# A gated cross-attention block: in the slot stage, maxima and sums over all slots are taken on VectorE, and the stage opens in another order

## The reference

```python
x = _layernorm(_layernorm(x)) * norm_g + norm_b           # 64 x 64 tokens
se = _layernorm(slot_embeds) * scale                      # 16 experts x 64 slots
logits = einsum('bnd,esd->bnes', x, se)
dispatch = softmax(logits, axis=1)                        # over the 64 tokens of a batch
combine = softmax(logits.reshape(B, N, -1), axis=-1)      # over all 1024 slots
slots = einsum('bnd,bnes->besd', x, dispatch)
gate = gelu(einsum('besd,edf->besf', slots, Wg) + bg)
up = einsum('besd,edf->besf', slots, Wu) + bu
eout = einsum('besf,efo->beso', gate * up, Wd) + bd
out = einsum('bns,bso->bno', combine, eout.reshape(B, E*S, -1))
x = x + tanh(g_ffn[0]) * out
```

## Time and profile before

| what | us |
|---|---|
| median of 3 runs (1504.78 to 1507.92) | 1505.92 |
| the profiled execution | 1507.57 |
| its span on the core | 1505.9 |
| PE busy | 1382.3 (92%) |
| DVE busy | 953.9 (63%) |
| ACT busy | 1013.6 (67%) |
| POOL busy | 524.3 (35%) |

### The profile page before, as it was taken

How to read it: one execution, slowest core, us unless ns; L and a number is a source line. 1 busy time by engine, 2 the same in 40 slices (tenths; PEclk the granted TensorE clock), 3 DMA queues, 4 the chain that set the end, 5 groups by cost and what they waited for, 6 DMA issues and landing times. The chain is left out here.

```text
span 1505.9 us, 33716 instructions
## 1 busy us (share of the span) xinstructions
PE 1382.3 (92%) x12029; PEld 1174.7 (78%) x12029; DVE 953.9 (63%) x2374; ACT 1013.6 (67%) x2019; POOL 524.3 (35%) x510
## 2 busy tenths in 40 slices
PE   5898699899999999999999999988999999877895
PEld 4887588788888888888888888876788888655673
DVE  6998766766766767677667666543455555644455
ACT  5887587577676776776776767647788888534442
POOL 3112355322322323223223223212235555545553
PEclk9999899999999999999999999999999999979998
DMA  8300100499930000000000000040000000122236
GB/s 222 85 1 1 58 2 1 87 183 84 114 17 2 2 1 2 2 2 1 2 2 1 2 2 2 1 114 15 1 31 15 16 16 19 31 63 69 70 92 175
DMA packets 124980, 60.46 MB, mean 40 GB/s; under 512 B 41945, under 2 KB 120241, under 8 KB 124690
## 3 DMA queue, kind: packets, MB, share of 16 engines
q1 hardware_dynamic: 120274, 48.92, 18.4%
q0 software_dynamic: 4544, 9.38, 1.9%
HBM read 28.84 MB, written 29.44 MB: 39 GB/s over the span
## 5 line engine op out<-in xcount | busy, mean ns | idle before, releaser
L1349 DVE SCALAR_TENSOR_TENSOR hidden<-psU,b_cols,gelu 128x512 f32<-128x512 f32 x256 | 191.6, 750 | 170.5 <-ACT gelu L1474 95.6
L1474 ACT ACTIVATE gelu<-psG,b_cols 128x512 f32<-128x512 f32 x256 | 176.5, 689 | 110.1 <-PE psG L142 97.2
L1296 POOL TENSOR_TENSOR combine_sum<-combine_sum,combineT 128x512 f32<-128x512 f32 x48 | 63.4, 1322 | 294.7 <-ACT combineT L1488 294.7
L1325 POOL TENSOR_TENSOR dispatchT<-dispatchT,dispatch_inv 128x512 f32<-128x512 f32 x64 | 67.8, 1060 | 232.5 <-DVE dispatch_inv L1453 232.5
L1608 PE MATMUL psU<-w_down,hidden 128*64 128x128 f32 x2048 | 123.4, 273 | 0.0
L1608 PE MATMUL psDown<-w_down,hidden 128*64 128x128 f32 x2048 | 122.7, 273 | 0.0
L1861 POOL TENSOR_TENSOR probs<-probs,row_sum 128x512 f32<-128x512 f32 x64 | 66.4, 1037 | 143.5 <-DVE row_sum L1974 142.6
L1608 PEld LDWEIGHTS psU<-w_down,hidden 128*64 128x64 f32 x2048 | 113.2, 137 | 1.3 <-issue 1.2
L1608 PEld LDWEIGHTS psDown<-w_down,hidden 128*64 128x64 f32 x2048 | 113.9, 137 | 0.1
L140 PE MATMUL psG<-slots_hi,w_gate_hi 128*128 128x512 f32 x256 | 106.4, 416 | 0.5 <-DVE slots_lo L1435 0.5
L2038 ACT ACTIVATE probs<-psS,neg_max 128x128 f32<-128x128 f32 x256 | 91.4, 385 | 22.8 <-DVE neg_max L1971 16.8
(11 more groups left out here) (406 smaller groups left out, 3624.8 us busy)
## 6 DMA issues: line engine op xcount, KB each, us to landing
sorted_x<-empty_rows SPq DMA_DIRECT2D x1, 12736.0 KB, 76.5
tile_rows<-sorted_x SPq DMA_DIRECT2D x78, 65.0 KB
sorted_x<-empty_rows SPq DMA_DIRECT2D x1, 4544.0 KB, 30.3
expert_ys<-expert_y SPq DMA_DIRECT2D x16, 256.0 KB, 3.7
x<-in_x SPq DMA_DIRECT2D x8, 256.0 KB, 5.9
ctx<-in_ctx SPq DMA_DIRECT2D x8, 256.0 KB, 5.9
w_gate_raw<-in_L_ffn_Wg SPq DMA_DIRECT2D x1, 2048.0 KB, 10.6
w_up_raw<-in_L_ffn_Wu SPq DMA_DIRECT2D x1, 2048.0 KB, 15.8
```

Source lines behind the costliest of these rows:

```text
L1325: pool.tensor_tensor(e[:], e[:], over(rb[:], SEQ, 2), ALU.mult).then_inc(s["eb_normed"], 1)
L1349: dve.scalar_tensor_tensor(hid[e][:, half, :], U[half][:], bcol[:, 1, 4 * ch + 2 * e + half:][:, 0:1], gel[half][:], ALU.add, ALU.mult).th ...
L1474: act.activation(gel[half][:], G[half][:], ACT.Gelu, bias=bcol[:, 0, 4 * ch + 2 * e + half:][:, 0:1]).then_inc(s["gelu"], 1)
```

## The change

- The maxima over slots: the four transposes, the four spreading matmuls and ScalarE's copy go. VectorE turns `top` in blocks of 32x32 and reduces each (`max_quadrants`, at the end of chunk 6), then brings the four quadrants of the partitions together, spreads the result over the quadrants and turns it back (`max_rows`, at the start of chunk 7).
- The sums over slots: the matmuls against ones go. VectorE turns and reduces `combine_sum` the same way (`sum_quadrants` before expert_out of chunk 7, `sum_inverse` near the end of that chunk).
- The waits of the next octet's first products for these results go.
- Scores 6 and 7 are both made in chunk 6, none in chunk 7.
- The next octet's tokens are turned at the start of chunk 1 (in octet 0: chunk 2), into psM.
- The opening: scores need no slots first; VectorE does the dispatch work before the running maxima, which come last, all seven (`first_top`), and `max_rows` for octet 0 stands in its chunk 0, behind the first two hidden. x_hat for octet 1 comes late in chunk 0 of octet 0.
- 24 of the statistics of 32 tiles go to the end of the first attention (four were there already), four stay in the stage.

```diff
+                    dve.wait_ge(s["bn"], OP * (OCTETS - 1))
+                    for t in range(OP, PAIRS - OP):
+                        dve.bn_aggr(c.stats[:, t, :], c.bn[:, t, :]).then_inc(s["late_aggr"], 1)
...
-    AHEAD = ((), (), (0,), (1, 2), (3,), (4, 5), (6,), (7,))
+    AHEAD = ((), (), (0,), (1, 2), (3,), (4, 5), (6, 7), ())
...
-            x_stats(c, dve, s["aggr"])
+            for t in range(PAIRS - OP, PAIRS):
+                dve.bn_aggr(c.stats[:, t, :], c.bn[:, t, :]).then_inc(s["aggr"], 1)
...
+            def by_quadrant(source, turned, n, op, count):
+                dve.transpose(turned[:], source).then_inc(s[n + "_turned"], 1)
+                need(dve, s[n + "_turned"], count)
+                dve.tensor_reduce(quad[n][:, 0, :], turned[:].rearrange("p (b i) -> p b i", i=32), AX.X, op
+                                  ).then_inc(s[n + "_quad"], 1)
+            def together(n, out, done, op, count):
+                need(dve, s[n + "_quad"], count)
+                for q in range(1, Q):
+                    last = dve.tensor_copy(quad[n][0:32, q, :], quad[n][32 * q:32 * (q + 1), 0, :])
+                last.then_inc(s[n + "_together"], 1)
+                need(dve, s[n + "_together"], count)
+                dve.tensor_reduce(out, quad[n][0:32].rearrange("p q b -> p b q"), AX.X, op).then_inc(s[done], 1)
+                need(dve, s[done], count)
+            def first_top():
+                for n in range(1, CH):
+                    need(dve, s["first_top"], n - 1)
+                    dve.tensor_tensor(top[:], raw[:, 0, :] if n == 1 else top[:], raw[:, n, :], ALU.max
+                                      ).then_inc(s["first_top"], 1)
+                dve.wait_ge(s["first_top"], CH - 1)
+            def max_quadrants(o):
+                need(dve, s["lb_max"], 8 * (o + 2))
+                need(dve, s["ct_sub"], 8 * (o + 1))
+                need(dve, s["mtok"], o + 1)
+                by_quadrant(top[:], mb, "max", ALU.max, o + 2)
+            def max_rows(o):
+                need(dve, s["mb_ready"], o + 1)
+                together("max", mtok[0:32, :], "mtok", ALU.max, o + 2)
+                for q in range(1, Q):
+                    last = dve.tensor_copy(mtok[32 * q:32 * (q + 1), :], mtok[0:32, :])
+                last.then_inc(s["max_spread"], 1)
+                need(dve, s["max_spread"], o + 2)
+                dve.transpose(mb[:].rearrange("p (b i) -> p b i", i=32), over(mtok[:], 32, 2)).then_inc(s["mb_ready"], 1)
+            def sum_quadrants(o):
+                need(dve, s["ct_summed"], 7 * (o + 1))
+                need(dve, s["max_turned"], min(o + 2, OCTETS))
+                need(dve, s["dtok"], o)
+                by_quadrant(total[:].rearrange("p t n -> p (t n)"), top, "sum", ALU.add, o + 1)
+            def sum_inverse(o):
+                need(dve, s["den"], o)
+                together("sum", dtok[0:32, :], "dtok", ALU.add, o + 1)
+                need(dve, s["x_new"], o)
+                for q in range(Q):
+                    last = dve.tensor_copy(ra[32 * q:32 * (q + 1), :],
+                                           dtok[0:32, :].rearrange("p (t q) -> p t q", q=Q)[:, :, q])
+                last.then_inc(s["den"], 1)
+                need(dve, s["den"], o + 1)
+                dve.reciprocal(ra[:], ra[:]).then_inc(s["den_inv"], 1)
+                need(dve, s["den_inv"], o + 1)
+                dve.tensor_scalar(ra[:], ra[:], c.gates[:, 1:2], None, ALU.mult).then_inc(s["den_gated"], 1)
...
+                    if ch == CH - 1 and has_head(o) and has_core(o):
+                        max_rows(o)
+                    if ch == turned_at(o) and has_head(o) and has_core(o):
+                        need(dve, s["lnT_hi"], o + 1)
+                        need(dve, s["lb"], 8 * (o + 1))
+                        dve.tensor_tensor(lnT[1][:], M[:, 1, :], lnT[0][:].bitcast(F32), ALU.subtract
+                                          ).then_inc(s["lnT_lo"], 1)
                     if not has_core(o):
+                        if exists(o, ch, 3):
+                            shift_dispatch(o, ch)
                         for n in ahead(o, ch):
                             column_max(o, n)
+                            if n == 5:
+                                slots_low(o, ch)
+                        if exists(o, ch, 3):
+                            sum_dispatch(o, ch)
+                        if ch == CH - 1:
+                            first_top()
+                            max_quadrants(o)
+                        continue
+                    if ch == 0 and has_head(o) and o > 0:
+                        x_hats(o)
+                    hidden(k, 0, ch, 0)
+                    hidden(k, 0, ch, 1)
+                    if ch == 0 and o == 0:
+                        max_rows(-1)
...
+                        if ch == CH - 1:
+                            sum_quadrants(o)
                         expert_out(k, 0, ch)
+                    if ch == 0 and o == 0:
+                        x_hats(o)
                     if exists(o, ch, 1):
+                        slots_low(o, ch)
+                    if has_core(o) and has_head(o) and ch == CH - 2:
+                        max_quadrants(o)
                     if has_core(o) and ch == CH - 1:
+                        sum_inverse(o)
                     if exists(o, ch, 3):
+                        sum_dispatch(o, ch)
...
+                    if ch == turned_at(o) and has_head(o) and has_core(o):
+                        need(pe, s["x_normed"], o + 1)
+                        need(pe, s["sl_lo"], 2 * (k + 1))
+                        for t in range(OP):
+                            last = pe.transpose(M1[:, t, :], xn[1 - par][:, t, :], c.ident[:])
+                        last.then_inc(s["tx"], 1)
...
-                first = isinstance(k, int) and ch == 0 and e == 0
-                if first:
-                    need(pe, s["mtok"] if half == 0 else s["mb_ready"], k // CH + 1)
+                if isinstance(k, int) and k == 0 and e == 0:
+                    pe.wait_ge(s["raw"], CH)
...
-                        for t in range(OP):
-                            last = pe.transpose(G0[:, t, :], top[:, t * P:(t + 1) * P], c.ident[:])
-                        last.then_inc(s["top_t"], 1)
...
-                        for t in range(OP):
-                            last = pe.matmul(U[0][:, t:t + 1], total[:, t, :], ones[:], start=True, stop=True)
-                        last.then_inc(s["den"], 1)
...
-                        for t in range(OP):
-                            last = pe.matmul(G[1][:, t * P:(t + 1) * P], mtok[:, t:t + 1].to_broadcast([P, P]), ident_r[:],
-                                             start=True, stop=True)
-                        last.then_inc(s["mb"], 1)
```

More of the change, by code:

```diff
@@ L1208, in stage_experts0 @@
         top = sb("top_over_chunks", [P, OT])
-        mtok, mb = sb("max_c", [P, OP], F32R), sb("max_c_row", [P, OT])
-        ident_r = sb("ident_rounded", [P, P], F32R)
+        quad = {n: sb(f"{n}_by_quadrant", [P, Q, OT // 32]) for n in ("max", "sum")}
+        mtok, mb = sb("max_c", [P, OT // 32]), sb("max_c_row", [P, OT])
+        dtok = sb("sum_c", [P, OT // 32])
         eb = [sb(f"dispatchT{i}", [P, OB, SEQ]) for i in range(2)]
@@ L1254, in second, with turned_at @@
             return any(n in group[1:] for group in AHEAD)
+        def turned_at(o):
+            return 2 if isinstance(o, int) and o == 0 else 1
         def score_bank(o, n):
@@ L1362, in column_max @@
                 if n == 1:
-                    need(dve, s["top_t"], o + 1)
-                if n > 0:
+                    need(dve, s["sum_quad"], o)
+                if n > 0 and has_core(o):
                     need(dve, s["lb_max"], j)
@@ new lines, in x_hats, with shift_dispatch @@
+            def x_hats(o):
+                need(dve, s["x_normed"], o)
+                for p in range(OP):
+                    t = 4 * (o + 1) + p
+                    last = dve.tensor_scalar(xh[:, p, :], c.x[:, t, :], c.stats[:, t, 0:1],
+                                             c.inv[:, bass.ds(t, 1)], ALU.subtract, ALU.mult)
+                last.then_inc(s["x_hat"], 1)
+            def shift_dispatch(o, ch):
+                k = o * CH + ch
+                n = (ch + 3) % CH
+                need(dve, s["raw"], k + 4)
+                need(dve, s["lb_max"], k + 4)
+                need(dve, s["td"], k + 2)
+                dve.tensor_tensor(eb[(ch + 1) % 2][:], raw[:, n, :].rearrange("p (b n) -> p b n", b=OB),
+                                  over(nm[:, n, :], SEQ, 2), ALU.add).then_inc(s["shifted"], 1)
@@ new lines, in sum_dispatch, with slots_low @@
+            def sum_dispatch(o, ch):
+                k = o * CH + ch
+                need(dve, s["eb_exp"], k + 4)
+                need(dve, s["eb_normed"], k + 3)
+                dve.tensor_reduce(rb[:], eb[(ch + 1) % 2][:], AX.X, ALU.add).then_inc(s["eb_sum"], 1)
```

(22 more changed lines are left out.)

130 lines of the change are left out of this document (41 added, 89 removed).

## The result

The changed kernel takes 1533.02 us (median of 4 runs, 1532.36 to 1533.81) against 1506.26 of the kernel before beside it: ratio 1.0176, interval 1.0163 to 1.0189, slower. 1515.4 was predicted, 1500 to 1530 given as the range. The profiled execution has a span of 1531.3 us against 1505.9: 25.4 us more, where I had 9.5.

What follows compares the result with a forecast made beforehand. VectorE's chain was taken to be as long as TensorE's work at the ends of octets 1 to 5. Ends 3.0, chunk 7 10.2, octet 6 -2.27, last sums -0.9, transposes -1.0, opening 0.5: +9.5, 1515.4 us, range 1500 to 1530.

Steps and rivals of the forecast that it cites:

- the stall of chunk 7: Chunk 7, seven times: TensorE waits for hidden behind VectorE's maxima work and copies held beside GpSimd, 1.45 us each, 10.2 together.
- the longer chain at an octet's end: From expert_out of chunk 7 to chunk 0's first hidden, VectorE's chain grows by 0.50 us, six ends, 3.0 together.
- the falls of the clock: Rival, 12%: after the new 2.7 us pauses TensorE's clock falls in each of five octets, 8.5 us, giving 1524.
- tokens' transposes: Turning the next octet's tokens at a chunk's start saves perhaps 0.15 us, seven times, 1.0 together.
- opening: Start of the slot block: b_cols comes at about the same time, +0.5 us, bounds -2 and +2.
- last sums: Eighth octet, without successor: only the sums' matmuls leave TensorE, 0.9 us saved.
- the end of octet 6: No x_hat follows since octet 7 prepares nothing, so the 2.27 us removed from TensorE is kept as gain.
- Removed from TensorE, 2.27 an end: Between chunk 7 and the next chunk 0, three removed groups cost TensorE 2.27 us in each of seven octets.
- The rival that no stall arises: Rival, 15%: VectorE's transposes and copies fit in chunk 7, only chunk 0 loses: -0.7 us, 1505.
- the one that TensorE stays the bound: Rival, 13%: TensorE's removed work is time saved, 17.3 us less, 1488.6.
- the one that x_hat gets free of GpSimd: Rival, 8%: x_hat no longer runs beside GpSimd, 3.47 becomes 1.11 us, five ends gain 2.3 each: 1504.
- The end of octet 0: The routing constants' chain starts from VectorE's row sums too, so this end also costs +0.50 us.

Runs made afterwards that it cites:

- e8: Changed kernel with its two new small buffers last and 480 unused bytes, so slots and hidden stand where the kernel before has them: 1530.18 us, ratio 1.0155.
- e9: e8, e2 and e3 together, x_hat behind the first expert_out of chunk 0, tokens turned at chunk 2 in every octet: 1501.91 us, ratio 0.9971.
- e3: Changed kernel with max_rows behind the first two hidden of chunk 7 instead of ahead of them: 1523.79 us, ratio 1.0097.
- e5: Changed kernel with the edits of e2, e3 and e4 together: 1514.6 us, ratio 1.004.
- e2: Changed kernel with sum_inverse moved from the end of chunk 7 into the next octet's chunk 0, just ahead of its use: 1517.18 us, ratio 1.0055.
- e1: Changed kernel with 32 unused bytes ahead of the slots, bringing slots and hidden to multiples of 64 bytes: 1535.74 us, ratio 1.0183.
- e4: Changed kernel with x_hat behind the first two hidden of chunk 0 instead of ahead of them: 1519.26 us, ratio 1.0067.
- e7: Kernel before with 96 unused bytes ahead of dispatchT, so operands stand at the changed kernel's addresses: 1515.04 us, ratio 1.0051.
- e10: Kernel before with 512 unused bytes ahead of dispatchT: ratio 1.0007.
- e11: Kernel before with 64 unused bytes ahead of dispatchT: ratio 1.0016.
- e12: Kernel before with 96 unused bytes between the slots and gelu, so only gelu, hidden and expert_out move: ratio 0.9998.
- e6: Kernel before, unedited, profiled a second time: 1506.39 us, ratio 0.9994.

## Why the prediction was wrong

The sign, the places and the two chains were right. What failed were two terms of the sum and one that was put at nothing: the stall of chunk 7 was 1.98 and not 1.45 us, the longer chain at an octet's end cost 1.03 and not 0.50 and also reached a wait that I had not listed, and the pitch of the products, which the sum did not have, cost 5.8. With the ends at their measured size alone the sum would have given about 1523; the pitch and the falls of the clock, which I had only as a rival, took it past 1530. The account of the profiled executions, by chunk lengths:

| part | predicted | measured |
|---|---|---|
| ends of octets, tokens' transposes included, at equal pitch | +9.9 | +17.5 |
| pitch of the products | none | +5.8 |
| clock after the pauses | 12% rival | +3.0 |
| opening, from the first score to the first chunk 1 | +0.5 | -0.1 |
| last sums | -0.9 | -0.2 |
| stages ahead and behind | none | -0.5 |
| sum | +9.5 | +25.5 |

Worked out, with e8 for the changed kernel at equal pitch: its chunks 6, 7 and 0 (13.11 + 13.66 + 15.19) less those of before (12.39 + 14.66 + 11.88) are 3.03 at an end where the clock holds; chunk 1 gives 0.31 back (12.11 against 12.42). That is 13.6 for five such ends; 1.0 for the end of octet 6, 2.7 for that of octet 0 and 0.2 for the transposes in octet 0's chunk 2 make 17.5 (for octet 0 with octet 1's chunk 0 as long as in the changed kernel, since e8's is 0.5 longer). Pitch: 0.7 in each of seven octets and 0.9 in the last. Stages: the first score comes 0.7 later (156.47 against 155.81), and from the first router transpose to the end it is 505.94 against 507.06. The spans to one digit give 25.4.

- **Removed from TensorE, 2.27 an end: right.** Before, chunk 7 takes 14.66 and a chunk with one score and no reduction 12.39: 2.27. In e9 chunks 7 and 0 take 23.65; before 26.54, of which 0.71 was the score: 2.18 less, with 0.2 to 0.3 of waiting left on either side.
- **VectorE's transposes and reductions, 0.71 and 0.60: right** (0.74 from 593.48 to 594.22, 0.60 to the row behind at 594.82). The copies beside GpSimd's normalization were held, as predicted from x_hat: 0.90 for three, 0.52 in e3 without it. The rule cited from the Trainium skill ("SBUF — State Buffer", section "SBUF: two separate sides") is borne out for small copies by e5, where a copy of 0.16 us lasted 1.17 and ended with GpSimd's instruction.
- **The stall of chunk 7, 1.45: too small by 0.5.** At equal pitch chunk 7 takes 13.66 (e8) where a chunk without score or wait takes 11.68: 1.98. The wait of 1.50 costs 1.78 of it, and the late expert_out, of which I had listed no consumer in this chunk, 0.15. `max_rows` alone is 1.71 (e3). The rival that no stall arises is out, as are the one that TensorE stays the bound and the one that x_hat gets free of GpSimd: it took 3.44 (610.58).
- **The chain of the sums, +0.50: the other term that was mis-sized.** From expert_out to the end of the first hidden I had 8.26 + 0.50; it is 605.36 to 614.65 = 9.29, so +1.03. I took 0.1 for a small instruction that waits for nobody; they start 0.17 apart (four in 0.68 and three in 0.52), and the chained ones 0.21 to 0.28. That is 1.9 from 607.27 to 609.18 where I had 1.44. The upper bound that I wrote beside it (1.1) was nearly the true value. The two terms close the account of an end: 1.98 + 1.03 = 3.01, where the chunks give 3.03 and I had 1.45 + 0.50.
- **A wait not listed.** My chain led to hidden alone. It passes expert_out, and TensorE's second group of psU products, which needs it, comes some 2.2 us after a chunk's first product, before the one that needs hidden. Hence 0.53 at 610.72, and 0.88 at the end of octet 6. There I had written that 2.27 is kept, since no x_hat follows. Chunk 0 took 12.94; 11.79 with the sums out of the way (e2). With the stall of chunk 7 I had -0.8 for this end; it cost 1.0.
- **The end of octet 0: too small in the same way.** Its wait for expert_out grew from 4.7 to 7.9 us, by the 2.27 that TensorE no longer works and the 1.0 of the chain; 5.9 in e2.
- **The tokens' transposes, 0.15 each, and the last sums, -0.9.** No row stood behind the 0.15; chunk 1 gave 0.31. The last sums gave 0.24 (e8, from octet 7's chunk 6 to the next stage), since the small instructions stand ahead of the last expert_out there too: VectorE has no gap from 1013.83 to 1016.45.
- **The clock: the rival came in part.** The same pause, 0.53 and then 2.35 us, ended with half the clock once and with the full one at other times (changed kernel, first 3 us after it; the number before the last two is the granted clock, 0.50 of 2.4 GHz being 1.2):

```profile
614.80:617.80 3.00, 3.00 (x7) 2.42 (x8) 1.89 (x3) 0.76 (x2) 2.20 (x2) 0.50 0.00 0
721.90:724.90 3.00, 2.95 (x19) 2.27 (x21) 2.39 (x4) 1.92 (x3) 2.34 (x2) 1.00 0.03 5
827.70:830.70 3.00, 2.99 (x21) 2.30 (x23) 2.38 (x4) 1.96 (x3) 2.29 (x2) 1.00 0.00 0
```

  Each fall cost 1.5 us (16.7 against 15.22), near my price (8.5 for five: 1.7). It came at two of the five ends here and in e8, at none in e1, at four in e3, after waits of the same two patterns (0.53 and 2.35, or 0.88 and 2.0). In e5 it followed a single wait of 1.77 to 1.79 us in two of five (0.61 and 0.69 over the 3.4 us behind it). In e2, e4 and e9, where no wait of these five ends is above 1.5 us, it never came. At the end of octet 0 it came before the change already (0.50 from 288 to 291, with the wait of 4.7 us), so it is no new cost there. What decides between equal waits stays open.
- **The pitch: not foreseen at all.** The diff replaces a rounded identity of 512 bytes by small buffers, which moves all that is allocated behind by 96 bytes. I read it as bookkeeping. The runs e7 and e8 tie 0.12 us of every quiet chunk to it, 5.8 us in all. Which rule of place is behind it stays open.
- **The opening: +0.5 came out, by luck.** b_cols comes at 177.70 (177.80 before) and the first chunk 1 starts 0.5 us later, as forecast. But the stage itself begins 0.7 later, and from its first score to the first chunk 1 it is 34.06 against 34.20. The stage also begins 0.6 to 1.5 later in e7, e10, e11 and e12, which only move buffers, so its start need not have to do with the new order.

The signs that I had named came almost all: waits of 1.50 and of 0.53 + 2.35 us, stretched copies. What did not hold was their cost: the ends of octets 1 to 5 took 2.7 us more at equal pitch and clock, 3.4 and more as measured, not some 2.

## What to carry to other kernels

- A reduction moved from a full engine to one with a third of its time free paid here only once its small instructions stood where they kept nobody waiting: put each behind the results that the full engine waits for, and check the next such result too. Here the order of four small groups, and where the slots stand, made the difference between 1.8% slower and 0.3% faster.
- Where two chains are equal within 0.1 us, the error of a sum of ten small instructions is the answer. Give unchained small instructions the duration of chained ones until a row shows otherwise, and trace a chain to every result that it delays. Where a small copy meets a GpSimd instruction, count the rest of that instruction once.
- When buffers are added or dropped, compare the addresses of what TensorE streams, or profile a quiet stretch: a chunk without any change is the control.

## What the hardware showed

- Products of 128x512 started 0.2286 us apart on average with the slots at one place and 0.234 apart with them and all behind 96 bytes further on, on the same instructions (e6 and e7, octet 7: 11.68 and 11.81 a chunk). Shifts by 64 and 512 bytes cost 0.03 and nothing a chunk.
- The first product after a wait was followed by the next only after 0.34 us instead of 0.23.
- VectorE's transpose of a 128x512 f32 tile in SBUF within blocks of 32 took 0.70 us, as much as an addition of that size.
- Copies of 32x16 f32 from one group of 32 partitions to another started 0.17 us apart. Beside a GpSimd addition one of three took 1.17 us, until the addition ended, and the other two 0.16 each.
- A pause of TensorE of 2.35 us that followed one of 0.53 was itself followed by half the clock at some ends and not at others, in one execution.
